# A two-layer decoder on one core: roundings on ScalarE, other slots in both layers' attentions, extra constant products at two stages' first steps

## The reference

```python
x = _layernorm(x + L0_attn(x))          # 16 heads; q, k, v and the output product are "bitlinear"
x = _layernorm(x + L0_xattn(x, ctx))    # rotary embedding, 16 heads over channels
x = _layernorm(x + L0_ffn(x))           # 8 experts, the best 2 per token, three layers with gelu
x = _layernorm(x + L1_attn(x))          # latent keys and values, 16 heads, causal
x = _layernorm(x + L1_xattn(x, ctx))
x = _layernorm(x + L1_ffn(x))           # product-key retrieval of 8 of 512 + gated MLP

def _bitlinear(x, w):                   # weights ternary, activations rounded to 8 bits per row
    sx = 127.0 / clip(max(abs(x), axis=-1), 1e-05)
    xq = clip(round(x * sx), -128, 127) / sx
    ...
```

## Time and profile before

| | us |
|---|---|
| median of 3 runs | 1553.11 (1552.55 to 1557.23) |
| the profiled execution | 1552.37 |
| its span, first to last instruction | 1550.6 |
| busy: PE, DVE, ACT, POOL | 1318.2, 987.7, 634.1, 439.0 |
| mean granted clock of TensorE | 0.924 |

### The profile page before, as it was taken

One profiled execution on the slowest core, in us unless ns is written; L12 is line 12 of the kernel. 1 busy time (PEld: TensorE's weight loads), 2 busy tenths in 40 slices (PEclk: granted clock), 3 DMA queues, 4 the chain that ended last, 5 costly groups with the idle time before them and its releaser, 6 DMA issues. The chain is left out here.

```text
span 1550.6 us, 29402 instructions
## 1 busy us (share of the span) xinstructions
PE 1318.2 (85%) x9140; PEld 879.0 (57%) x9235; DVE 987.7 (64%) x3391; ACT 634.1 (41%) x1421; POOL 439.0 (28%) x611
## 2 busy tenths in 40 slices
PE   3578999999999927899999965788899976899997
PEld 1345666666665414555566633456666643688886
DVE  6478888888888452222222223588888752678886
ACT  2224555555555511222222223366666542343331
POOL 2252433433432001111111013665665420101100
PEclk8678999999999968999999986799999997899999
DMA  3343444444433054611111114875555420200000
GB/s 101 62 82 56 82 70 71 82 62 81 77 62 45 10 183 134 211 32 34 35 35 34 28 39 83 176 136 113 122 128 121 101 62 22 77 1 15 15 1 28
DMA packets 165944, 112.75 MB, mean 73 GB/s; under 512 B 32786, under 2 KB 155922, under 8 KB 165664
## 3 DMA queue, kind: packets, MB, share of 16 engines
q1 hardware_dynamic: 146816, 96.63, 27.9%
q0 software_dynamic: 3408, 9.31, 2.5%
q10 hardware_dynamic: 15568, 4.93, 1.5%
HBM read 46.48 MB, written 12.45 MB: 38 GB/s over the span
## 5 line engine op out<-in xcount | busy, mean ns | idle before, releaser
L931 ACT ACTIVATE first_probs<-pair 128x512 f32<-128x512 f32 x320 | 189.2, 597 | 160.4 <-PE pair L446 156.0
L1095 DVE CUSTOM_DVE_ANT_0 first_masked<-bank,kept_mask_q 128x256 bf16<-128x256 f32 x512 | 189.6, 417 | 16.8 <-PE bank L431 16.0
L431 PE MATMUL bank<-kept_stack_cross 96*128 96x256 bf16 x768 | 152.7, 282 | 14.9 <-DVE first_negmax_x L1095 9.8
L446 PE MATMUL pair<-kept_stack_cross 98*128 98x256 bf16 x768 | 148.6, 275 | 4.6 <-ACT second_probs L1961 1.5
L1961 ACT ACTIVATE second_probs<-pair 128x512 f32<-128x512 f32 x192 | 112.1, 597 | 69.2 <-PE pair L446 66.2
L1483 PE MATMUL pair<-kept_w,experts_hidden_t 128*128 x312 | 140.3, 592 | 0.0
L1524 ACT ACTIVATE experts_hidden_t<-bank,kept_b 128x128 f32<-128x128 f32 x156 | 44.4, 367 | 184.0 <-PE bank L1458 184.0
L1438 POOL DMA_INDIRECT experts_expert_rows<-x_mid,kept_row_of x39 | 37.1, 951 | 273.2 <-PE bank L1450 247.0
L431 PEld LDWEIGHTS bank<-kept_stack_cross 96*128 96x128 bf16 x768 | 66.1, 101 | 65.6 <-issue 24.1
L1483 PEld LDWEIGHTS pair<-kept_w,experts_hidden_t 128*128 128x128 f32 x312 | 59.3, 190 | 74.1 <-issue 74.1
L446 PEld LDWEIGHTS pair<-kept_stack_cross 98*128 98x128 bf16 x768 | 73.9, 99 | 42.0 <-ACT second_probs L1961 3.6
(11 more groups left out here) (452 smaller groups left out, 2990.3 us busy)
## 6 DMA issues: line engine op xcount, KB each, us to landing
kept_stack_self<-first_parts_a SPq DMA_DIRECT2D x128, 64.0 KB
kept_w<-in_L_ffn_W SPq DMA_DIRECT2D x16, 512.0 KB, 7.5
kept_w<-in_L_ffn_W SPq DMA_DIRECT2D x8, 1024.0 KB, 6.9
kept_stack_self<-second_parts_a SPq DMA_DIRECT2D x128, 64.0 KB, 3.6
kept_stack_cross<-first_parts_x_k SPq DMA_DIRECT2D x96, 64.0 KB
kept_stack_cross<-first_parts_x_q SPq DMA_DIRECT2D x96, 64.0 KB
kept_stack_cross<-second_parts_x_k SPq DMA_DIRECT2D x96, 64.0 KB
kept_stack_cross<-second_parts_x_q SPq DMA_DIRECT2D x96, 64.0 KB
```

What stands on the lines that cost most here:

```text
L431: mm = pe.matmul(out, q, k, start=mask is None, stop=True, skip_group_check=True)
L446: mm = pe.matmul(out, k, q, start=mask is None, stop=True, skip_group_check=True)
L931: act.activation(probs[i % RING][:, :], key_bank[i % 2][:, :], ACT.Exp, scale=att.scale).then_inc(probs_made, 1)
L1095: ins = dve.tensor_tensor_reduce(masked[(2 * i + a) % 16][:, :], score_bank[i % 2][:, a * D:(a + 1) * D], t["mask_q"][:, a, :], -1.0, 3.0e ...
```

## The change

Four edits go together.

- In the first layer both roundings move from DVE to ACT: two activations each (Identity with the row's scale and ROUND as bias, then Identity with -ROUND as bias), the two constants in a new tile `shift`. ACT waits between the two for its own result, and for `scales_made` or the new `qo_made` before them. `row_scales_of` on DVE waits for `whole_made`, since ACT now reads the scales.
- The first layer's slots: other numbers for most steps. The lanes of scores stay as they are.
- The second layer's slots: the same.
- `keep_clock`: PE multiplies the bf16 identity by a constant tile of 128x512 into a bank that nobody reads then. 10 such products stand ahead of the experts' first tile, 8 ahead of the retrieval's first transposes, and 3 ahead of each of `turn_rows` and `route` for its first four blocks.

```diff
+def keep_clock(pe, t, bank, times):
+    for _ in range(times):
+        pe.matmul(bank[:, :], t["ident16"][:, :], t["causal_q"][:, :], start=True, stop=True, skip_group_check=True)
...
         slots = Slots(20)
-        OWN_SCORES, CROSS_SCORES, OWN_KEYS, CROSS_KEYS = 0, ((44, 4), (48, 12)), 11, ((67, 4), (75, 12))
-        LOAD_ROWS, ROW_SCALES, ROUND_ROWS, TURN_ROWS, COPY_ROWS, MAKE_QK, SCALE_QK, MAKE_V, COPY_V, TURN_QK, COPY_QK = -29, -27, -22, -19, -18, -16, -16, -15, -13, -11, -11
-        SPLIT_SELF, STACK_FIRST, STACK_SECOND, STACK_THIRD = -11, -9, -8, -8
-        OWN_TWO, TURN_OWN_MAXIMA, OWN_ROWS, OWN_VALUES, COPY_OUT, TURN_OUT, OWN_HEADS, HEAD_SCALES, ROUND_HEADS = 3, 5, 6, 15, 17, 19, 21, 24, 24
-        TURN_HEADS, COPY_HEADS, MAKE_O, OWN_SUM, ROOT_A, OWN_END = 26, 26, 28, 28, 29, 29
+        OWN_SCORES, CROSS_SCORES, OWN_KEYS, CROSS_KEYS = 0, ((44, 16),), 11, ((67, 4), (75, 12))
+        LOAD_ROWS, ROW_SCALES, ROUND_ROWS, TURN_ROWS, COPY_ROWS, MAKE_QK, SCALE_QK, MAKE_V, COPY_V, TURN_QK, COPY_QK = -31, -26, -22, -18, -18, -16, -16, -14, -14, -12, -12
+        SPLIT_SELF, STACK_FIRST, STACK_SECOND, STACK_THIRD = -11, -10, -8, -6
+        OWN_TWO, TURN_OWN_MAXIMA, OWN_ROWS, OWN_VALUES, COPY_OUT, TURN_OUT, OWN_HEADS, HEAD_SCALES, ROUND_HEADS = 3, 6, 7, 16, 16, 19, 19, 22, 23
+        TURN_HEADS, COPY_HEADS, MAKE_O, OWN_SUM, ROOT_A, OWN_END = 26, 26, 27, 27, 28, 28
...
-        STORE_ROWS, TURN_X2, COPY_X2, MAKE_LOGITS, KEEP_LOGITS = 107, 108, 108, 110, 113
+        STORE_ROWS, TURN_X2, COPY_X2, MAKE_LOGITS, KEEP_LOGITS = 115, 109, 111, 113, 115
...
+            def round_heads(b):
+                if b >= 1:
+                    act.wait_ge(oq_turned, b)
+                act.wait_ge(qo_made, b + 1)
+                act.activation(whole_o[:, :], heads_a[:, :], ACT.Identity, scale=qo[:, 2:3], bias=shift[:, 0:1]).then_inc(whole_o_made, 1)
+                act.wait_ge(whole_o_made, b + 1)
+                act.activation(oq[:, :], whole_o[:, :], ACT.Identity, bias=shift[:, 1:2]).then_inc(oq_made, 1)
...
+                    dve.wait_ge(whole_made, b)
...
-                round_rows(dve, x0[b % 3][:, :], qs, whole[:, :], xq[:, :]).then_inc(xq_made, 1)
...
-                round_rows(dve, heads_a[:, :], qo, whole_o[:, :], oq[:, :]).then_inc(oq_made, 1)
...
+            keep_clock(pe, t, ps[6], 10)
             turn_rows(0)
...
         slots = Slots(12)
-        GATHER, LOAD_ROWS, COMBINE, COMBINED_MOMENTS, ROOT_M, KEEP_ROWS, LAY_X3, TURN_X3, COPY_X3 = -32, -32, -24, -23, -23, -21, -20, -19, -19
-        MAKE_LATENT, LATENT, ROOT_L, LATENT_END, TURN_LATENT, COPY_LATENT, MAKE_KEYS_VALUES, COPY_KEYS_VALUES = -17, -17, -13, -13, -12, -12, -11, -11
-        SPLIT_FIRST, STACK_FIRST, SPLIT_REST, SPLIT_SECOND, STACK_SECOND, SPLIT_LAST, STACK_THIRD = -10, -8, -10, -8, -6, -6, -3
+        GATHER, LOAD_ROWS, COMBINE, COMBINED_MOMENTS, ROOT_M, KEEP_ROWS, LAY_X3, TURN_X3, COPY_X3 = -38, -35, -24, -24, -24, -23, -23, -19, -19
+        MAKE_LATENT, LATENT, ROOT_L, LATENT_END, TURN_LATENT, COPY_LATENT, MAKE_KEYS_VALUES, COPY_KEYS_VALUES = -17, -16, -16, -15, -12, -12, -11, -11
+        SPLIT_FIRST, STACK_FIRST, SPLIT_REST, SPLIT_SECOND, STACK_SECOND, SPLIT_LAST, STACK_THIRD = -11, -3, -10, -8, -3, -8, -3
...
-        STORE_ROWS, TURN_X5, COPY_X5, MAKE_QUERIES, COPY_QUERIES, STORE_QUERIES = 69, 71, 71, 73, 73, 73
+        STORE_ROWS, TURN_X5, COPY_X5, MAKE_QUERIES, COPY_QUERIES, STORE_QUERIES = 73, 71, 71, 73, 73, 78
...
+            keep_clock(pe, t, gate_bank[0], 8)
             pe.wait_ge(loaded, LOADED)
...
             for m in range(TOGETHER):
+                keep_clock(pe, t, gate_bank[0], 3)
                 turn_rows(0, m)
+                keep_clock(pe, t, gate_bank[0], 3)
                 route(0, m)
```

More of the change, by code:

```diff
@@ L598, in first_layer_attentions @@
         stats_a, stats_x = sb("stats_a", [P, 10]), sb("stats_x", [P, 10])
+        shift = sb("shift", [P, 2])
         x2_t = sb("x2_t", [P, KT, P])
@@ L606, in first_layer_attentions @@
             [sem(f"{n}_{u}") for u in range(3)] for n in ("x0_loaded", "kv_loaded", "stack_q_arrived", "stack_k_arrived", "maxrows_x_arrived"))
-        scales_made = sem("scales_made")
+        scales_made, whole_made, shift_made = sem("scales_made"), sem("whole_made"), sem("shift_made")
+        whole_o_made, qo_made = sem("whole_o_made"), sem("qo_made")
         xq_made, xq_turned, xq_copied = sem("xq_made"), sem("xq_turned"), sem("xq_copied")
@@ new lines, in first_layer_attentions @@
+        TURN_HEADS, COPY_HEADS, MAKE_O, OWN_SUM, ROOT_A, OWN_END = 26, 26, 27, 27, 28, 28
+        LOAD_CONTEXT, MAKE_CROSS_K, ROTATE_K, SPLIT_KEYS, STACK_KEYS = 6, 15, 16, 19, 28
+        MAKE_CROSS_Q, ROTATE_Q, SPLIT_QUERIES, STACK_QUERIES = 30, 33, 36, 44
+        MAKE_CROSS_V, COPY_CROSS_V, CROSS_TWO, TURN_CROSS_MAXIMA, CROSS_ROWS = 58, 60, 60, 61, 61
+        CROSS_VALUES = (74, 82, 84, 88)
+        COPY_CROSS_OUT, CROSS_RECIPS, LAY_RECIPS, SPREAD_SUMS, CROSS_HEADS, MAKE_Y, CROSS_SUM, ROOT_X, CROSS_END = 88, 94, 94, 98, 98, 100, 100, 103, 103
@@ L931, in exponential, with round_rows_of @@
                 act.activation(probs[i % RING][:, :], key_bank[i % 2][:, :], ACT.Exp, scale=att.scale).then_inc(probs_made, 1)
+            def round_rows_of(b):
+                if b == 0:
+                    act.wait_ge(shift_made, 1)
+                else:
+                    act.wait_ge(xq_turned, b)
+                act.wait_ge(scales_made, b + 1)
+                act.activation(whole[:, :], x0[b % 3][:, :], ACT.Identity, scale=qs[:, 2:3], bias=shift[:, 0:1]).then_inc(whole_made, 1)
+                act.wait_ge(whole_made, b + 1)
+                act.activation(xq[:, :], whole[:, :], ACT.Identity, bias=shift[:, 1:2]).then_inc(xq_made, 1)
+            def round_heads(b):
[5 more added lines that the diff above has]
+                act.activation(oq[:, :], whole_o[:, :], ACT.Identity, bias=shift[:, 1:2]).then_inc(oq_made, 1)
             def copy_rows(b):
@@ L1016, in _ @@
                     copy_out(b)
+                if (b := slots.batch_at(s, ROUND_HEADS)) is not None:
+                    round_heads(b)
                 if (b := slots.batch_at(s, COPY_HEADS)) is not None:
@@ L1020, in _ @@
                     copy_x2(b)
+                if (b := slots.batch_at(s, ROUND_ROWS)) is not None:
+                    round_rows_of(b)
                 if (b := slots.batch_at(s, COPY_ROWS)) is not None:
@@ L1122, in head_scales @@
                 row_scales(dve, heads_a[:, :], qo)
-                dve.tensor_scalar(qo[:, 3:4], t["mw4"][:, 3:4], qo[:, 0:1], None, ALU.mult)
-            def round_heads(b):
-                if b >= 1:
-                    dve.wait_ge(oq_turned, b)
-                dve.drain()
-                round_rows(dve, heads_a[:, :], qo, whole_o[:, :], oq[:, :]).then_inc(oq_made, 1)
+                dve.tensor_scalar(qo[:, 3:4], t["mw4"][:, 3:4], qo[:, 0:1], None, ALU.mult).then_inc(qo_made, 1)
             def own_sum(b):
@@ L1198, in _ @@
                     head_scales(b)
-                if (b := slots.batch_at(s, ROUND_HEADS)) is not None:
-                    round_heads(b)
                 if (b := slots.batch_at(s, OWN_SUM)) is not None:
@@ L1216, in _ @@
                     row_scales_of(b)
-                if (b := slots.batch_at(s, ROUND_ROWS)) is not None:
-                    round_rows_of(b)
 def load_expert(queue, d, t, e):
@@ new lines, in second_layer_attentions @@
+        SPLIT_FIRST, STACK_FIRST, SPLIT_REST, SPLIT_SECOND, STACK_SECOND, SPLIT_LAST, STACK_THIRD = -11, -3, -10, -8, -3, -8, -3
+        OWN_TWO, TURN_OWN_MAXIMA, OWN_ROWS, OWN_VALUES, COPY_OUT, TURN_OUT, OWN_HEADS, TURN_HEADS, COPY_HEADS, MAKE_O, OWN_SUM, ROOT_A, OWN_END = 3, 5, 5, 14, 15, 17, 17, 19, 19, 20, 21, 22, 23
+        LOAD_CONTEXT, SPLIT_KEYS, STACK_KEYS, SPLIT_QUERIES, STACK_QUERIES, TURN_CONTEXT, COPY_CONTEXT, CROSS_TWO, TURN_CROSS_MAXIMA, CROSS_ROWS = 12, 15, 23, 23, 24, 40, 40, 43, 44, 44
```

19 lines of the change are left out of this document (5 added, 14 removed).

## The result

| | before | after |
|---|---|---|
| median | 1555.17 us (4 runs, 1552.55 to 1562.25) | 1574.25 us (4 runs, 1570.84 to 1578.98) |
| ratio | | 1.0112, interval 1.0081 to 1.0143 |
| profiled execution, its span | 1552.37, 1550.6 | 1574.87, 1572.9 |

What follows compares the result with a forecast made beforehand. PE was taken to bound the first layer's attentions, DVE a close second. First layer -11, second layer -6, experts -1.5 and retrieval -1 sum to -19.5 from 1552.4, giving 1533 us, range 1514 to 1556.

Steps and rivals of the forecast that it cites:

- up to 0.6 a window: Second layer: cost of the layernorm's power queued on POOL behind the query splitting, with KEEP_ROWS and LAY_X3 following at -23.
- The bound for the second layer (+8): Second layer: worst case if SyncE's self-attention stacks, all issued at slot -3, come late and PE waits for them.
- the -6 of the sum: Second layer's new slots: net gain of 6 us, mainly from PE's removed waits for the latent; best case -14.
- -5 for -11: First layer: the prediction's -11 us is 14 full windows at 0.8 us less each, bounds 0 to -19.
- The L718 and L796 waits: First layer: PE's weight-load waits for ACT's q and k and DVE's rounded heads would go, saving 0.67 us a window.
- 0.8 a window: First layer: 0.67 us from removed waits plus 0.13 from earlier row maxima, bounds 0 and 1.33.
- the slower rival: First layer, ACT's dense slots 3 to 9: 1.5 us of stall a window, +21 us, time 1565; chance 0.11.
- the 1.2 of the sum: First layer: one rounding pair on ACT takes 1.2 us, 1.03 for two activations plus 0.2 wait; bounds 0.77 and 1.9.
- -1.8 for -1: Retrieval's constants: predicted net -1 us, from +2.7 ahead, -1.8 for four blocks and -1.9 for gate products.
- the experts' first product as forecast: Experts' constants: first product 1.98 us instead of 3.78 at the raised clock; the term was -1.5 us in all.
- The rival that the clock stays low in the retrieval: Retrieval: clock remains 0.50 despite the constants, +10.7 us in place of -1, time 1544.5; chance 0.07.
- The chance of slower, 0.12: Whole kernel: probability given to a slower result, against 0.77 faster and 0.11 same.

Runs made afterwards that it cites:

- kernel 3: The changed kernel with the gathers of the experts' rows (GATHER) back at slot -32 from -38; 1549.08 us, ratio 0.9946.
- kernel 5: The changed kernel with GATHER back at -32 and KEEP_ROWS and LAY_X3 back at -21 and -20; 1544.46 us, ratio 0.9940.
- 10: On top of kernel 3, the first layer's cross queries (MAKE_CROSS_Q) at slot 32 instead of 30; 1573.89 us, ratio 1.0139.
- kernel 1: The changed kernel with the second layer's slot numbers as before the change; 1550.59 us, ratio 0.9971.
- 4: The changed kernel with KEEP_ROWS and LAY_X3 back at -21 and -20, gathers left at -38; 1556.12 us, ratio 0.9984.
- 2: The kernel before with only the second layer's new slot numbers; 1579.71 us, ratio 1.0154.
- 11: The kernel before with only the ten constant products ahead of the experts' first tile; 1553.63 us, ratio 0.9984.
- 12: The kernel before with only the retrieval's constant products; 1552.37 us, ratio 0.9986.
- 6: The kernel before with both roundings on ScalarE, all slots of before and no constants; 1608.77 us, ratio 1.0348.
- 8: On top of 6, HEAD_SCALES moved from 24 to 22 and ROUND_HEADS from 24 to 23; 1565.90 us, ratio 1.0088.

## Why the prediction was wrong

**The step that failed: what POOL has ahead of the power.** The prediction saw that `ROOT_M` stands behind `SPLIT_QUERIES` and that `KEEP_ROWS` follows one slot later, and priced it at "up to 0.6 a window". It took the 3.6 us from 1153.98 to 1157.54 as they were. Left out was the moved step itself: `GATHER` goes from -32 to -38, in slots of a window from 4 to 10, which puts two gathers, 2.3 us of GpSimd (1130.18 to 1132.50), right ahead of that splitting (now 11), and with them an idle time inside it. That idle time stood in the trace of before, at another place, where nobody waited for it; the waits view of before, 1040 to 1200 us, has

```profile
POOL second_rest_x_k L376 <- issue: 13.3, 8, 2.9
```

against 0.2 us and less for the splitting of the queries. It is behind the gathers in both kernels: behind -32 stands the splitting of the keys, behind -38 that of the queries. What GpSimd stands at is the `drain` between the first two instructions of the splitting; the one at the place shown above (count, length in ns, start in us):

```profile
L375 POOLq DRAIN  x1: 3967/3967/3967, 1131.7 to 1131.7; - x1
```

It ends at 1135.64, 0.12 us after the last of the 32 semaphore increments with which the two gathers' rows land (1135.52). So do all 11 such drains of after and 9 of the 10 of before (the tenth 0.45 us), and 113 of the 121 in all the traces that have them; none ends before it. By this the drain, meant for the splitting's own result, also waits until the rows of the gathers are there. So the power has to wait for the issue of the gathers and for their landing. Price: 2.4 us for each of DVE's 11 waits (26.8 in all), 3.2 for each of PE's 10, and behind most of these a stretch at the low clock; the stage is 25 us longer. The prediction followed the moved stores and stacks through SyncE's queue, not this one through GpSimd's. The bound for the second layer (+8) was too low for the same reason: it was made from SyncE's stacks, and the loss was +25.

**The second layer's gain: the wait is gone, the gain smaller.** The L1815 wait is gone with `LATENT_END` at -15. With the cause of the loss removed (kernels 3, 5 and 10) the stretch from the last tile of the experts to the last sum of the second layer takes 405.6 to 412.3 us, mean 409; with the old slots 407.7 to 414.8 in eight traces, mean 411. So -2 by single traces whose ranges overlap; by the ratios kernels 3 and 5 are 4 and 5 us under kernel 1, which differs from them in this layer's slots alone. That is -2 to -5 for the -6 of the sum; in kernel 5 the windows in the middle are 19.1 to 19.9, not shorter than before (18.4 to 21.1), and what is gained is gained when the stage runs empty (its last windows 16.0 and 14.8 for 17.1 and 16.4). PE waits for row maxima (where they are turned, L417) and for `x_perm` (9.7 us in 10, 1020 to 1280) in place of the latent.

**The first layer: right in sign, -5 for -11.** `first_sum_x` last starts at 550.4 to 553.6 in the five traces with the whole first layer changed and nothing added to it (after and kernels 1, 3, 4, 5), mean 552.1, and at 555.6 to 557.8 in the four with the old one (before and kernels 2, 11, 12), mean 556.8: -4.7. The L718 and L796 waits are gone, as the prediction had it, and PE's busy share rose from 95.2 to 96.9 (forecast 97 to 98), but the full window fell from 28.1 to 27.85 only. By the period that the prediction used, `sum_a` from the first to the last batch, it is 27.6 to 27.1 (75.9 to 483.0) for the 26.8 forecast; 4.8 of the 7.4 us that it gains in 15 windows come from the first three windows, whose filling the prediction took at zero. The term "0.8 a window" left out the new wait at L829, 0.96 a window. Its place is that of the slower rival, ACT's slots 3 to 9: it was right that the copy of q and k and the cross output's DMA collide there, wrong that this makes the layer slower. Its 1.5 us of stall a window came as 0.96, and other waits had gone. `qo_made` costs next to nothing (one wait of 1.4 us from 100 to 500 us), since `HEAD_SCALES` was moved two slots up; kernels 6 and 8 show what the wait costs without that, 40 us. The prediction said that it "belongs to the rival" and did not price the two numbers that defuse it.

**The roundings' cost.** ACT's two activations take 590 and 508 ns in after (557 and 470 in the sum). The second has one per-row operand like the row of 470, but a bias for the scale, another source and a bf16 output; which of these makes the 38 ns no run separates. The wait for the own result, taken at 0.2 us, is 0.03, so a pair takes 1.13 us for the 1.2 of the sum. ACT's busy share went to 62.9 (forecast 64), DVE's from 88.7 to 84.5, by 4 points for the forecast 6.

**The constants: right for the retrieval, open for the experts.** Retrieval -1.8 for -1, with +2.6 ahead for +2.7 (the first block's rows 5.35 us behind PE's first product for 2.72) and 2.04 a block for 2.2; the experts' first product as forecast, its gain lost in the spread of the stage. The rival that the clock stays low in the retrieval did not come: PEclk is 0.86 from 1342 to 1350 and 1.00 after it. Of the Trainium skill's rule in TensorE: Matmul & The Clock Gate, Part 4: PE-mode transpose, that the full clock does not engage for transposes: here two transposes take 0.38 us between constant products, for 0.69 at the low level, so this trace doesn't bear the rule out where such products stand around them; what transposes alone would do no run shows.

**The bounds.** Without the failed step the sum is right in sign and some 10 us too good: kernel 5 gains 0.6%, 9 us, for the 19.5 of the forecast. The chance of slower, 0.12, hung on one mechanism in one stage; the second layer, in which some thirty numbers were changed, had only one bound of its own.

## What to carry to other kernels

Write out the in-order queue of every engine through one window, with the moved steps in their new places and each wait's idle time in it, before a moved step is priced: the dear thing about the gather was not its own time but who stood behind it. An idle time that costs nothing where it is has to be moved along with its cause, and a step that waits for another engine needs a slot or two of distance from what it waits for (two numbers of distance were worth 40 us here). On GpSimd, no step that someone waits for should stand behind a `drain` that follows freshly issued gathers; whether a wait for the splitting's own semaphore in the drain's place would do as well, no kernel tried. Two edits that lose alone may gain together, so a change of many slot numbers has to be measured in both directions, each part alone and each part taken back.

## What the hardware showed that was not expected

- A `drain` on GpSimd that follows two indirect DMAs holds until their rows have landed. In the 11 places of after and the 10 of before where it holds, it ends 0.12 us (once 0.45) after the last increment of the gathers' semaphore, and GpSimd has stood idle for 1.2 to 3.7 us. Elsewhere the same drain costs 0.16 to 0.34 us in all but one case of these two traces (1.0). Before, the splitting of the keys stood behind the gathers (with one other instruction between them; 13.3 us in 8), after, that of the queries, and with the gathers seven slots ahead of the queries the idle time is gone there (2.7 us in 8 in kernel 3).
- The eight waits of PE of 2.5 to 3.9 us from 1040 to 1240 in after were each followed by a stretch at the low level of the clock; the waits of some 2 us were followed by one in some places and not in others: behind 1.96 us in the experts of after it fell, behind 2.02 at the same instruction of before it did not.
- Ten constant products at the low level take 4.42 us, after which the first real product runs at the high level.
